# Another order of TensorE's work in the attention steps of a gated cross-attention block

## The reference

```python
Q = (layernorm(x) @ Wq).reshape(16, 100, 4, 4, 32) / sqrt(32)
K, V = (ctx @ Wk).reshape(16, 361, 4, 32), (ctx @ Wv).reshape(16, 361, 4, 32)
scores = einsum('bqghd,bkgd->bghqk', Q, K) + slope * (key - query)
w = softmax(where(mask, scores, lowest), axis=-1)
x = x + tanh(g_xattn) * (einsum('bghqk,bkgd->bqghd', w, V) @ Wo)
x = x + tanh(g_ffn) * ffn(layernorm(x))    # gate, up, silu, rms norm, down; int8-like rounding
```

## Time and profile before

| what | us |
|---|---|
| median of 3 runs (lowest to highest) | 561.91 (557.28 to 563.38) |
| profiled execution | 564.89 |
| its span, first to last instruction | 562.9 |
| PE busy | 490.2 |
| DVE busy | 366.9 |
| ACT busy | 335.5 |
| POOL busy | 233.2 |

### The profile page before, as it was taken

The page is one execution under the profiler, slowest core; times in us unless marked ns, Lnnn a source line. Parts: engine busy times, 40 slices in busy tenths (PEclk is TensorE's granted clock), DMA queues, the critical chain, the costliest instruction groups (busy, mean ns, idle before and its releaser), DMA issues.

```text
span 562.9 us, 8377 instructions
## 1 busy us (share of the span) xinstructions
PE 490.2 (87%) x2898; PEld 306.3 (54%) x2898; DVE 366.9 (65%) x672; ACT 335.5 (60%) x565; POOL 233.2 (41%) x251
## 2 busy tenths in 40 slices
PE   2599599879994998999999999769999999999984
PEld 1599599879961444444444444234555455555431
DVE  3785257247651778888888895156777777777750
ACT  0335646446561676566667665557777777777662
POOL 1000000000005666766553670056666767766650
PEclk9999979998997999899999999978999999999987
DMA  7877977999429798778776812001333333333222
GB/s 184 252 240 265 355 244 255 293 285 284 159 47 213 229 193 187 171 163 200 164 153 167 198 39 96 0 1 37 76 76 76 75 75 75 75 75 76 66 56 47
DMA packets 55690, 83.35 MB, mean 148 GB/s; under 512 B 30782, under 2 KB 42254, under 8 KB 53734
## 3 DMA queue, kind: packets, MB, share of 16 engines
q1 hardware_dynamic: 50470, 57.72, 40.6%
q0 software_dynamic: 3456, 12.58, 8.6%
q10 hardware_dynamic: 1728, 12.58, 6.4%
HBM read 57.29 MB, written 9.85 MB: 119 GB/s over the span
## 4 chain that ended last, share of the span: by engine, by line
PE 62%; DVE 14%; DMA 8%; ACT 8%; issue 5%; SPq 2%; POOLq 0%; DVEq 0%; ACTq 0%
PE wide L1289 10%; PE bank L1123 10%; PE wide L1123 7%; PE bank L1299 6%; PE bank L1216 6%; PE wide L1192 6%; PE bank L1206 5%; PE bank L1164 5%; PE bank L1219 5%; DVE row_max L921 4%; DMA ct<-ctx_t 3%; ACT p_t L668 3%; DMA wq_f<-wq 2%; DMA qs<-nm_t 2%; DMA xb<-x 1%
## 5 line engine op out<-in xcount | busy, mean ns | idle before, releaser
L921 DVE TENSOR_REDUCE row_max<-wide 100x2 f32<-100x722 f32 x128 | 110.2, 902 | 40.0 <-PE wide L1192 39.9
L668 ACT ACTIVATE p_t<-bank 121x400 f32<-121x400 f32 x192 | 92.4, 504 | 58.2 <-PE bank L1206 54.7
L1289 PE MATMUL wide<-w_q,xq 128*128 128x512 bf16 (+1 forms) x416 | 95.9, 384 | 0.9 <-ACT xq L715 0.8
L531 POOL TENSOR_TENSOR z<-h,lnw 128x512 f32<-128x512 f32 (+1 forms) x52 | 66.5, 1279 | 34.7 <-DVE h L1031 27.0
L1289 PEld LDWEIGHTS wide<-w_q,xq 128*128 128x128 bf16 (+1 forms) x416 | 40.1, 100 | 51.9 <-issue 6.4
L489 POOL DMA_DIRECT2D quant_in<-w_ffn x24 | 14.3, 595 | 126.6 <-DVE small L912 120.1
L1206 PE MATMUL bank<-qs,ks 103*121 103x400 f32 x144 | 50.5, 382 | 10.8 <-DMA qs<-nm_t 7.6
L1299 PE MATMUL bank<-w_q,yq 128*128 128x512 bf16 (+1 forms) x208 | 52.6, 401 | 7.9 <-DMA yq<-y_int 7.4
L1192 PE MATMUL wide<-ks,qs 101*100 101x362 f32 x192 | 49.6, 345 | 7.9 <-DVE row_max L921 6.5
L763 ACT ACTIVATE act<-wide,small 128x512 f32<-128x512 f32 (+1 forms) x52 | 35.1, 679 | 35.3 <-PE wide L1289 23.2
L1164 PE MATMUL bank<-wv_f,ct 128*121 128x128 f32 x384 | 48.3, 286 | 4.4 <-DMA ct<-ctx_t 4.4
(11 more groups left out here) (137 smaller groups left out, 920.0 us busy)
## 6 DMA issues: line engine op xcount, KB each, us to landing
quant_in<-w_ffn POOLq DMA_DIRECT2D x24, 512.0 KB, 6.9
ct<-ctx_t SPq DMA_DIRECT2D x16, 722.0 KB, 8.8
abs_b<-w_ffn ACTq DMA_DIRECT2D x8, 1024.0 KB, 8.7
ks<-k_all SPq DMA_DIRECT2D x36, 181.0 KB
q_scratch<-qhl SPq DMA_DIRECT2D x16, 400.0 KB, 5.2
qs<-q_scratch SPq DMA_DIRECT2D x12, 400.0 KB
abs_a<-w_ffn ACTq DMA_DIRECT2D x4, 1024.0 KB, 7.9
xb<-x SPq DMA_DIRECT2D x12, 256.0 KB, 2.8
```

The source lines that it names most:

```text
L531: nc.gpsimd.tensor_tensor(z[par][0:rows, c], h[0:rows, c], lnw[0:rows, c], ALU.mult).then_inc(z_done, 1)
L668: nc.scalar.activation(p_t[:, j, :], bank[j % 2][0:KT, 0:HQ], ACT.Exp).then_inc(exp_done, 1)
L921: nc.vector.tensor_reduce(row_max[b % 2][:, 2 * u:2 * u + 2], wide[u % 2][0:SQ, :, 0:SK], AX_X, ALU.max).then_inc(s_maxed, 1)
L1289: mm = nc.tensor.matmul(wide[j % 2][0:rows, m, :], xq[:, c, 0:rows], w_q[:, m * C + c, 512 * j:512 * j + 512], start=(c == 0), stop=(c == ...
```

## The change

The table `BEHIND` is rewritten. Slot 0 keeps two transposed scores and the transpose of the maxima; the values and sums of key tiles 0 and 1 stand together in slot 3 and those of tile 2 in slot 6; the remaining transposed scores come two to a slot, those of the next batch from slot 5 on. Each operation still runs once in a step. Nothing else in the program changes: the waits, and the order of the other engines, are as before.

```diff
--- before.py
+++ after.py
@@ -76,14 +76,14 @@
 
 
 NORMALISE_BEHIND = {3: (0, 1), 5: (2,)}
-BEHIND = {0: [("t", 2, 4), ("t", 2, 5), ("pv", 2, 0), ("turn", 1, 0), ("t", 2, 6), ("t", 2, 7)],
-          1: [("t", 2, 8)],
-          2: [("t", 2, 9), ("t", 2, 10)],
-          3: [("t", 2, 11), ("pv", 2, 1)],
-          4: [("t", 1, 0)],
-          5: [("t", 1, 1), ("t", 1, 2), ("pv", 2, 2)],
-          6: [("t", 1, 3)],
-          7: []}
+BEHIND = {0: [("t", 2, 4), ("t", 2, 5), ("turn", 1, 0)],
+          1: [("t", 2, 6), ("t", 2, 7)],
+          2: [("t", 2, 8), ("t", 2, 9)],
+          3: [("pv", 2, 0), ("pv", 2, 1)],
+          4: [("t", 2, 10), ("t", 2, 11)],
+          5: [("t", 1, 0), ("t", 1, 1)],
+          6: [("pv", 2, 2), ("t", 1, 2)],
+          7: [("t", 1, 3)]}
 
 
 def flamingo_block(nc, x, ctx_t, mask, gates, wq, wk, wv, wo, w_ffn, ln_w, alibi_q, alibi_k, eye, out):
```

## The result

The changed kernel takes 611.21 us in the median (605.96 to 615.45), the kernel before 562.45 (557.28 to 563.38) in the same session: a ratio of 1.088, 95% interval 1.081 to 1.095. It is slower by 49 us. The profiled execution took 612.05 us, its span is 610.1.

A forecast was written before the change was run, and what follows sets the result against it. The prediction took each step as bound by a loop through TensorE and ScalarE. Order without clock effect 26.5 plus clock 20.2 gave 46.7 us on the 561.9 median: 608.6, predicted as 608, range 584 to 622.

The forecast's parts named there:

- The step at the full clock, 13.71 us: Attention step replayed over TensorE and ScalarE: 13.7 instead of 11.66 us, 2.05 more, without any clock effect.
- The pauses that the replay named: TensorE around slot 0: about 0.7 us before unit 5, about 1.8 us between transpose and slot-1 scores.
- The clock, 1.6 us a step: TensorE's clock falls in nearly every step, catching slots 2 and 3 scores and slot 3's first run; +20.2 us net.
- The page's rule: Clock falls need one unbroken idle gap longer than any pause here; if it holds, the clock-stays-up case is the outcome.
- the clock stays up: Rival for the attention steps: pauses too short one by one to lower the clock; cost 25.1 us, time 587; chance 0.25.
- 24.6 - 1.6 + 0.8: Middle steps: twelve at 2.05 us more; VectorE's split of wo falls in slack, -1.6; ScalarE's split joins the chain, +0.8.
- 12 x 1.6 - 1.4: Clock price of 1.6 us in each middle step, less 1.4 for the fall at 226.8 the old order already paid.
- The start, -0.7: TensorE's stall for the maxima's DMA: slot 5 and batch-0 units move ahead of it; slot-1 scores about 186.9 against 187.59.
- The end, +3.4: Slot-1 scores at 331.73 to unit 5 of the last batch: 24.5 instead of 21.1 us by the same replay.
- The late DMA: Rival: `load_qk` issues later, so the maxima's DMA is late, up to 2.7 us a step; about 626 us; chance 0.08.
- Faster, since the chain is not the wait: Rival: ScalarE runs ahead by 2.7 us or more, TensorE's work sets an 11.0 us step; 12 us faster, 550; chance 0.03.
- The two terms: Whole kernel: 26.5 us from the new order without any clock effect, and 20.2 us from clock falls.

The follow-up runs named there:

- filled kernel: Changed kernel plus nine small float32 matmuls, results unused, behind the transpose of the maxima, before the slot-1 scores; 592.2 us, ratio 1.056 to the kernel before.
- with one entry moved: Kernel before with only the values and sums of key tile 0 moved from slot 0 to slot 3; 603.92 us, ratio 1.074.
- the first of the three tries: Kernel before, slot 0 kept, later slots regrouped: next batch's units 0 and 1 in slot 3, key tile 2's run ahead of unit 2; 561.29 us, ratio 1.003.
- another kernel: Changed kernel with the values and sums of key tile 0 moved back from slot 3 to slot 0; 579.53 us, ratio 1.032 to the kernel before.

## Why the prediction was right

The forecast was 608 us against 611.2 measured. Three fences for what follows: TensorE of the changed kernel behind the stall of step 2, TensorE in the last attention steps, and the landing of the maxima's DMAs.

```profile
176.91 1.02 PE L1206 MATMUL bank<-qs,ks 103*121 103x400 f32 x2 [4.89 <-DMA qs<-nm_t]
...
178.47 1.56 PE L1216 MATMUL bank<-p_t,v_all 121*32 121x400 f32 x8
...
181.29 0.69 PE L1206 MATMUL bank<-qs,ks 103*121 103x400 f32 x1
...
186.03 0.90 PE L1192 MATMUL wide<-ks_late,qs_late 101*100 101x362 f32 x2 [0.91 <-ACT nm_t L580]
```

```profile
373.31 0.71 PE L1192 MATMUL wide<-ks_late,qs_late 101*100 101x362 f32 x2 [1.98 <-ACT nm_t L580]
...
398.91 0.44 PE L1206 MATMUL bank<-qs_late,ks_late 103*121 103x400 f32 x1 [0.69 <-ACT p_t L668]
```

```profile
DMA to landing us min/median/max: 1.7/2.2/9.2
```

- *The step at the full clock, 13.71 us.* The filled kernel shows 13.73. The pauses that the replay named are there: 1.8 forecast, 1.72 measured, ended by the copy; 0.7 forecast, 0.74 measured. ScalarE idles 4.02 us beside the double run, where the text said over 2.
- *The clock, 1.6 us a step.* All twelve steps have a mean below 1.00. From the slot-1 scores of step 3 to those of step 15 are 373.31 - 186.03 = 187.3 us; the filled kernel takes 169.4 for the same steps (187.21 to 356.57), so the clock costs 1.5 a step. But no step costs that: the regular ones take 14.65 and 16.1 us by turns, 0.9 and 2.4 more than 13.73. The forecast knew of no such turns. That 1.6 is close to their mean is in part luck.
- *The page's rule.* The Trainium skill's "TensorE: Matmul & The Clock Gate", section "HAM oscillation — how this bites in real kernels", puts falls down to one unbroken gap longer than any pause of these steps. The clock fell in the regular steps behind pauses of 1.72 and 0.74 us, and with one entry moved behind pauses of 0.78 us and less. The measurement decides, against that section's rule: the case "the clock stays up" (587) did not come. The filled kernel is that case made on purpose, at 592.
- *The middle in sum.* The twelve steps took 144.1 us before (187.59 to 331.73) and 187.3 now: +43.1. The forecast had 24.6 - 1.6 + 0.8 for the chain there and 12 x 1.6 - 1.4 for the clock, together 41.6. In the filled kernel they take 25.2 us more than before, where 22.4 was worked out for a clock that stays up (24.6 - 1.6 + 0.8 - 1.4).
- *The start, -0.7: did not come from the order.* From the end of the stall to the slot-1 scores of step 3 are 9.04 us before (178.55 to 187.59) and 9.12 after (176.91 to 186.03). The work that the order moved ahead of the stall was saved, but the run behind the stall took 2.82 us (178.47 to 181.29), all of it at the low clock, and the chain from unit 2 took 4.74 instead of 4.56. The slot-1 scores come 1.6 us earlier all the same. That is not the order's doing: this execution is 2.0 us ahead of the other already at the first transposed scores (159.30 against 161.30), before anything that the order moves. Counted from there, the start costs 0.4 us.
- *The end, +3.4.* Slot-1 scores to unit 5 of the last batch take 25.6 us against 21.1, +4.5, with a fall of the clock in it. In the filled kernel they take 24.6 (356.57 to 381.19), where 24.5 was worked out.
- *The late DMA.* It did not come: 2.2 us in the median against 2.7, and unit 0 waits for it only in step 2. In the first of the three tries, where unit 0 was moved ahead, it was a wait of 1.54 us in one step.
- *Faster, since the chain is not the wait.* Out by the row that names the copy. But its sentence "nothing in the rows gives those 2.7 us, since exponential 3 stands behind the copies" has the wrong reason: with exponential 3 ahead of them the time is 612.1, the same. ScalarE's work between unit 2 and the copy of the maxima adds up, in whatever order.

The two terms one by one. With the clock held up, the new order costs 592.2 - 561.1 = 31.1 us in that run's session, where 25.1 was worked out for this case: low by 6. Between the profiled executions it is 27.9. Of that excess, 2.8 us lie in the twelve steps, mostly in the two with the fall that is left, which take 15.4 and 14.2 us; the last 3 are the distance between the profiled execution of the kernel before and its median. The clock costs what is left of the 48.8 us, 17.7, where 13.5 x 1.6 = 21.6 was worked out: high by 4. The errors have opposite signs, which flatters the sum.

## What to carry to other kernels

In a hand-written order on one engine, as here, a long independent operation is worth most beside the longest chain on another engine: find the instruction that every step waits for, follow its chain back, and put the long operation there, not where it is tidy to bunch it. Replay one step with distances read from the timeline before moving anything; here that gave the step's length at the full clock to 0.1 us (13.71 worked out, 13.73 measured). And count the clock of TensorE as part of the price of a pause: when work thins out in each period, some filler that keeps it up can pay for itself.

## What the runs showed of the hardware

The granted clock fell to 0.50 with no pause of TensorE longer than 1.72 us just before: behind 0.74 and 1.72 us in the regular steps of the changed kernel, behind 0.78 us and less with one entry moved. Nearly the same two pauses, 0.74 and 1.68 us, with a run of values and sums between them, left it at 1.00 in one step of another kernel. Nine useless matmuls in the pause of each step kept it at 1.00 but for one fall and made the kernel 19 us faster; three, in a pause of 0.72 us, kept it up but for two falls and were worth 20 us.
